# Key and value products in slot 2, the next batch's query product in slot 11, and gate logits from eight columns of the cross products

## What is computed

```python
x = layernorm(x + self_attention(x))      # 16 query heads of 16, one key and value head of 16 for all
qp, kp = proj(x), proj(context)           # proj: two linear maps with biases, one after the other
x = layernorm(x + softmax(qp @ kp.T / 16 + mask) @ context)     # 120 context rows a batch
gate = softmax(x @ Wg.T)                  # 8 experts; the best 2 of each row, scaled to sum 1
x = layernorm(x + sum(gate[e] * (glu(x @ W1[e].T + b1[e]) @ Wo.T + bo) for e in best2))
```

## Time and profile before

| | |
|---|---|
| median of 3 runs | 1420.98 us (1415.15 to 1421.51) |
| the profiled execution | 1420.46 us, span 1418.7 us |
| mean granted TensorE clock | 0.974 |
| first batch's maxima begin | 44.9 us |
| steady steps (7 to 31) | 21.8 us each |
| last exponential of self-attention ends | 786.1 us |
| first expert tile on TensorE | 837.6 us |
| last tile transposed, rows combined | 1242.7 us, 1410.3 us |

### The profile page before, as it was taken

The page is one execution under the profiler, slowest core; times in us unless marked ns, Lnnn a source line. Parts: engine busy times, 40 slices in busy tenths (PEclk is TensorE's granted clock), DMA queues, the critical chain, the costliest instruction groups (busy, mean ns, idle before and its releaser), DMA issues.

```text
span 1418.7 us, 30148 instructions
## 1 busy us (share of the span) xinstructions
PE 1274.8 (90%) x7734; PEld 900.7 (63%) x7735; DVE 1147.8 (81%) x3145; ACT 747.3 (53%) x1740; POOL 642.5 (45%) x978
## 2 busy tenths in 40 slices
PE   6997999999999999999988569999999999968886
PEld 4443555655556555555553357888888888858886
DVE  0565889898888988988986658888888888869998
ACT  1245777777777787777776212233233223314444
POOL 3011354455444554555445323333333333348886
PEclk9998999999999999999999679999999999989999
DMA  7656667667676675775655853433443344379995
GB/s 163 166 111 125 113 151 172 149 163 149 158 157 140 146 163 135 157 138 145 157 129 195 290 215 129 135 130 129 134 135 129 130 134 135 133 271 330 332 335 194
DMA packets 182817, 237.57 MB, mean 167 GB/s; under 512 B 21376, under 2 KB 144256, under 8 KB 176960
## 3 DMA queue, kind: packets, MB, share of 16 engines
q1 hardware_dynamic: 158864, 169.50, 47.3%
q0 software_dynamic: 17488, 55.02, 10.3%
q10 hardware_dynamic: 6368, 11.89, 2.4%
HBM read 138.34 MB, written 98.30 MB: 167 GB/s over the span
## 4 chain that ended last, share of the span: by engine, by line
PE 62%; DVE 17%; issue 9%; DMA 5%; ACT 4%; POOL 1%; SPq 1%; DVEq 0%; ACTq 0%; POOLq 0%
PE psO L623 6%; PE psS L730 5%; PE psHb L1399 5%; PE psHb L1396 5%; PE psHb L1395 4%; PE psHa L1395 4%; PE psHa L1396 4%; PE psHa L1399 4%; PE psB L652 4%; PE psT L740 4%; DVE negmax L1031 3%; DVE x2in L1591 3%; PE psX L1419 2%; DVE gt_lo L1567 2%; PE psA L612 2%
## 5 line engine op out<-in xcount | busy, mean ns | idle before, releaser
L1031 DVE TENSOR_REDUCE negmax<-psS 128x2 f32<-128x512 f32 x512 | 350.7, 688 | 94.6 <-PE psS L730 77.0
L870 ACT ACTIVATE probs<-psT 128x512 f32<-128x512 f32 x512 | 304.0, 599 | 161.0 <-PE psT L740 143.3
L1476 ACT ACTIVATE sig<-hb 128x512 f32<-128x512 f32 x135 | 85.6, 634 | 286.6 <-DVE hb L1549 286.6
L730 PE MATMUL psS<-kstack,qstack 96*128 96x256 bf16 x1024 | 195.2, 273 | 31.3 <-DVE kstack L1129 15.6
L740 PE MATMUL psT<-qstack,kstack 99*128 99x512 bf16 x512 | 194.8, 383 | 4.4 <-ACT probs L870 4.3
L1358 POOL DMA_INDIRECT g_rows<-g,slot x135 | 134.7, 998 | 69.8 <-issue 66.5
L730 PEld LDWEIGHTS psS<-kstack,qstack 96*128 96x128 bf16 x1024 | 93.1, 104 | 90.2 <-DVE negmax L1031 27.4
L482 POOL DMA_INDIRECT lists<-x,slots x128 | 128.6, 1005 | 33.9 <-issue 30.1
L623 PE MATMUL psO<-probs,vaug 128*32 128x512 f32 x1024 | 139.1, 616 | 0.4 <-ACT probs L870 0.4
L1560 DVE SCALAR_TENSOR_TENSOR g<-g,xe,sig 128x512 f32<-128x512 f32 x135 | 101.5, 752 | 26.0 <-DVE g L1556 16.6
L1549 DVE TENSOR_TENSOR hb<-psHb,b 128x512 f32<-128x512 f32 x135 | 93.4, 692 | 33.1 <-issue 28.9
(11 more groups left out here) (207 smaller groups left out, 2956.4 us busy)
## 6 DMA issues: line engine op xcount, KB each, us to landing
rows<-g_rows SPq DMA_DIRECT2D x32, 1024.0 KB, 8.1
qstack<-q_parts SPq DMA_DIRECT2D x192, 128.0 KB
xe<-lists SPq DMA_DIRECT2D x135, 133.0 KB, 2.1
q_parts<-qpart SPq DMA_DIRECT2D x32, 384.0 KB
sums<-x SPq DMA_DIRECT2D x32, 264.0 KB
x2in<-sums SPq DMA_DIRECT2D x32, 264.0 KB, 4.7
xt<-in_x_t SPq DMA_DIRECT2D x32, 256.0 KB
part_raw<-in_f_t SPq DMA_DIRECT2D x32, 256.0 KB, 5.0
```

The costliest lines, as they stand in the source:

```text
L730: last = mm(psS[:, u % 2, hh * S:(hh + 1) * S], qstack[0:KROWS, b1.s4, 2 * hp + hh, c * P:(c + 1) * P], kstack[0:KROWS, b1.s4, :], start=T ...
L870: nc.scalar.activation(probs[:, u % PT, :], psT[:, u % 2, :], ACT.Exp, scale=SELF_SCALE).then_inc(sm["exp_done"], 1)
L1031: v.tensor_reduce(negmax[:, b1.s2, 2 * hp:2 * hp + 2, c], psS[:, u % 2, :].rearrange("p (h k) -> p h k", h=2), AX.X, ALU.max, negate=True) ...
```

## The change

The gate's logits are rstd2 times y2 · wgc, where wgc is wg less its column means, since the norm takes the mean of y2 away and scales it. And y2 is x1 plus the cross-attention's output. So the new kernel never transposes x2. It puts wgc into eight more columns of `keymap`, so that the cross scores' products also give x1 · wgc; it multiplies the context with wgc (two small matmuls on a newly loaded `ctxt`, slot 9) and puts that into eight more columns of `ctxv`; and y2 comes with its eight unscaled logits as columns 256 to 263. Products, copies and norm halves get these slots:

- The pipeline starts one step earlier, and its last step, which only dispatched, is gone: 39 steps, -1 to 37. In step t, q is batch t+1.
- Keys and values of batch t in slot 2, copies in slots 3 and 4, krest in slot 3, third part in slot 7.
- The query of batch t+1 in slot 11, cast and rest in slot 12, the split on POOL behind the rstd of batch t-4 and ahead of mask_b. SP loads xt for t+1 first of all, then stores the query, later loads the stacks.
- The norm to x2 is cut in halves, slots 5 and 6. Gate on VectorE from slot 6 (maxima) and 7 (indices) to 15; exponentials in slots 8 and 9, with rstd2 as scale; counts into psO instead of psB.
- The product with the context uses psA for the first half and psB for the second.
- When draining, the gate runs in slots 1 to 15 and a batch is dispatched and stored at the end of the same step.

The core of the diff; the semaphores' names, the tiles' new sizes (`keymap`, `x1`, `y2`, `ctxv` are eight columns wider, `x2t` and `logits` are gone) and the count per batch of rstd2_ready (4 instead of 3) are left out:

```diff
-        for n in range(B + 7):
+        for n in range(-1, B + 6):
...
+    def count_bank(t):
+
+        return psB if draining(t) else psO[:, 0]
...
-            load_xt(t)
+            load_xt(t.back(-1))
...
+            if active(t):
+                wait(sp, "q1_cast", done(t))
+                wait(sp, "q_split", done(t, 2))
+                sp.dma_start(dram["q"][t.s2].rearrange("t (c p) s -> p t c s", p=P), qpart[:, t.s2]
+                             ).then_inc(sm["q_stored"], 16)
+            if active(t.back(7)) and t.n <= B + 1:
+                store_x2(t.back(7))
...
+                sp.dma_start(ctxt[:, b.s2], io["context_t"][:, b.n * SC:(b.n + 1) * SC].rearrange("(c p) k -> p c k", p=P)
+                             ).then_inc(sm[f"ctxt_loaded{b.s2}"], 16)
...
+            if active(t.back(6)) and draining(t):
+                store_x2(t.back(6))
...
+        def scale_max(b):
+
+            wait(pool, "rstd2_ready", 4 * b.n + 2)
+            pool.tensor_tensor(gneg[:, b.s2], uneg[:, b.s2], rstd2[:, b.s2], ALU.mult).then_inc(sm["rstd2_ready"], 1)
...
+                wait(pool, "gate_exp", done(b6.back(2)))
+                rstd(b6, "var2_ready", mv2, vare2, nmean2, rstd2, shift2, "rstd2_ready", per=4)
+                scale_max(b6)
...
+            late = active(b7) and t.n <= B + 1
+            if late:
                 dispatch(b7, 0)
...
+            if active(q):
+                wait(pool, "q_rest", done(q))
+                wait(pool, "q_stored", done(q.back(2), 16))
+                pool.tensor_tensor(qpart[:, q.s2, 1], qrest[:, q.s2], one_c[:, :].unsqueeze(2).to_broadcast([P, DC, S]),
+                                   ALU.mult).then_inc(sm["q_split"], 1)
+                wait(pool, "q_split", 2 * q.n + 1)
+                pool.tensor_tensor(qpart[:, q.s2, 2], qrest[:, q.s2], qpart[:, q.s2, 1], ALU.subtract
+                                   ).then_inc(sm["q_split"], 1)
...
+            if active(b6) and draining(t):
+                dispatch(b6, 0)
+                dispatch(b6, 1)
...
+            for k in range(DC):
+                mm(psT[:, 0, DC:DC + E], ones[:, :], wg[:, k, :], start=k == 0, stop=k == DC - 1)
...
-        bank_b = {"q_projected": ("q_rest", 0, 1, 1), "x2_transposed": ("x2t_copied", 6, 1, 1),
-                  "gate_scored": ("gate_link", 6, 7, 1), "cprob_transposed": ("cprobt_copied", 5, 1, 1),
-                  "kv_projected": ("k_rest", 0, 1, 1), "counted": ("slot_link", 6, 3, 1)}
+        bank_b = {"kv_projected": ("k_rest", 0, 1, 1), "cprob_transposed": ("cprobt_copied", 5, 1, 1),
+                  "q_projected": ("q_rest", -1, 1, 1), "cross_out": ("y2_ready", 5, 1, 1)}
...
+            if w == 0:
+                wait(pe, "slot_link", 3 * (b.n - 4) + 1)
...
-                if u == 5 and active(b6):
-                    wait(pe, "x2_ready", done(b6))
-                    bank_read(bank_b, t, "x2_transposed")
-                    for c in range(QC):
-                        for k in range(DC):
-                            last = nc.tensor.transpose(psB[:, k * S + c * P:k * S + (c + 1) * P],
-                                                       x2[:, b6.s2, c, k * P:(k + 1) * P], ident[:, :])
-                    last.then_inc(sm["x2_transposed"], 1)
...
-                if u == 7 and active(b6):
-                    wait(pe, "x2t_copied", done(b6))
-                    bank_read(bank_b, t, "gate_scored")
-                    for c in range(QC):
-                        for k in range(DC):
-                            last = mm(psB[:, c * E:(c + 1) * E], x2t[:, b6.s2, k, c * P:(c + 1) * P], wg[:, k, :],
-                                      start=k == 0, stop=k == DC - 1)
-                    last.then_inc(sm["gate_scored"], 1)
...
+                            last = mm(psA[:, c * (SC + E):(c + 1) * (SC + E)], x1t[:, b5.s2, k, c * P:(c + 1) * P],
+                                      keymap[:, k, b5.n, :], start=k == 0, stop=k == DC - 1)
+                    last.then_inc(sm["cross_scored"], 1)
...
+                    if draining(t):
+                        wait(pe, "slot_link", 3 * b6.n + 1)
+                    for c in range(QC):
+                        nc.tensor.transpose(psB[0:SC, c * P:(c + 1) * P], cprob[:, b5.s2, c, :], ident[:, :])
+                    wait(pe, f"ctxt_loaded{b5.s2}", 16 * b5.half + 16)
+                    for k in range(DC):
+                        last = mm(psB[0:SC, S:S + E], ctxt[:, b5.s2, k, :], wgc[:, k, :],
+                                  start=k == 0, stop=k == DC - 1)
+                    last.then_inc(sm["cprob_transposed"], 1)
+                if u == 11 and active(q):
+                    wait(pe, f"xt_loaded{q.s2}", 16 * q.half + 16)
+                    bank_read(bank_b, t, "q_projected")
...
+                    bank_read(bank_b, t, "cross_out")
                     for c in range(QC):
-                        last = mm(psA[:, c * D:(c + 1) * D], cprob_t[:, b5.s2, c * P:(c + 1) * P], ctxv[:, b5.s2, :],
+                        last = mm((psA, psB)[c][:, 0:D + E], cprob_t[:, b5.s2, c * P:(c + 1) * P], ctxv[:, b5.s2, :],
...
-                    bank_read(bank_b, t, "counted")
+                    if draining(t):
+                        bank_read(bank_b, t, "cprob_transposed")
+                    else:
+                        wait(pe, "att_copied", 2 * b3.n + 1)
+                    count = count_bank(t)
...
-                    wait(act, "q_projected", done(t))
-                    wait(act, "q_stored", done(t.back(2), 16))
-                    copy(qpart[:, t.s2, 0].rearrange("p c s -> p (c s)"), psB[:, :]).then_inc(sm["q1_cast"], 1)
-                if u == 4 and active(b6) and not draining(t):
+                    wait(act, "kv_projected", done(t))
+                    wait(act, "pv_done", 4 * (t.n - 3))
+                    wait(act, "scored", UNITS * (t.n - 3))
+                    copy(vaug[:, t.s4, :, 0:DK], psB[:, S:S + QC * DK].rearrange("p (c d) -> p c d", c=QC))
+                    copy(kstack[0:KROWS, t.s4], psB[0:KROWS, 0:S]).then_inc(sm["kv_cast"], 1)
+                if u == 4 and active(t):
+
+                    wait(act, "k_rest", done(t))
+                    copy(kstack[32:64, t.s4], krest[32:64, t.s2])
+                    copy(ksmall[64:80, t.s2], krest[64:80, t.s2]).then_inc(sm["k_mid"], 1)
+                if u in (5, 6) and active(b6) and not draining(t):
                     wait(act, f"x2_stored{b6.s2}", 16 * b6.half)
...
                     wait(act, f"dispatched{b6.s2}", 2 * QC * 16 * b6.half)
-                    norm(x2, rstd2, shift2, y2, b6, "rstd2_ready", "x2_ready")
...
-                    copy(x2t[:, b6.s2].rearrange("p c s -> p (c s)"), psB[:, :]).then_inc(sm["x2t_copied"], 1)
+                    norm(x2, rstd2, shift2, y2, b6, "rstd2_ready", "x2_ready", 4, u - 5)
+                if u in ((6,) if draining(t) else (8, 9)) and active(b6):
+                    wait(act, "gate_max", done(b6))
+                    wait(act, "rstd2_ready", done(b6, 4))
+                    wait(act, "comb_ready", done(b6.back(2)))
+                    for c in range(QC) if draining(t) else (u - 8,):
+                        nc.scalar.activation(gexp[:, b6.s2, c, :], y2[:, b6.s2, c, D:D + E], ACT.Exp,
+                                             scale=rstd2[:, b6.s2, c:c + 1], bias=gneg[:, b6.s2, c:c + 1],
+                                             accum_out=gsum[:, b6.s2, c:c + 1])
+                        last = nc.scalar.activation(gtop[:, b6.s2, c, :], top[:, b6.s2, c, 0:2], ACT.Exp,
+                                                    scale=rstd2[:, b6.s2, c:c + 1], bias=gneg[:, b6.s2, c:c + 1])
...
+                    copy(ctxv[:, b5.s2, D:D + E], psB[0:SC, S:S + E])
                     copy(cprob_t[:, b5.s2], psB[0:SC, 0:S]).then_inc(sm["cprobt_copied"], 1)
...
+                if u == 12 and active(q):
+                    wait(act, "q_projected", done(q))
+                    wait(act, "q_stored", done(q.back(2), 16))
+                    copy(qpart[:, q.s2, 0].rearrange("p c s -> p (c s)"), psB[:, :]).then_inc(sm["q1_cast"], 1)
...
+            v.scalar_tensor_tensor(wgc[:, :, :], psT[:, 0, DC:DC + E].unsqueeze(1).to_broadcast([P, DC, E]), -1.0 / D,
+                                   wg[:, :, :], ALU.mult, ALU.add)
+            for k in range(DC):
+                v.scalar_tensor_tensor(keymap[:, k, :, SC:SC + E],
+                                       psT[:, 0, DC:DC + E].unsqueeze(1).to_broadcast([P, B, E]), -1.0 / D,
+                                       wg[:, k, :].unsqueeze(1).to_broadcast([P, B, E]), ALU.mult, ALU.add)
...
+                    v.tensor_tensor(gneg[:, b6.s2], uneg[:, b6.s2], rstd2[:, b6.s2], ALU.mult
+                                    ).then_inc(sm["rstd2_ready"], 1)
...
+            if at(6, 1):
+                for c in range(QC):
+                    last = v.max(top[:, b.s2, c, :], y2[:, b.s2, c, D:D + E])
```

(46 more changed lines are left out.)

360 lines of the change are left out of this document (144 added, 216 removed).

## The result

| | before | changed |
|---|---|---|
| median | 1417.52 us (10 runs, 1409.81 to 1421.96) | 1427.31 us (10 runs, 1422.19 to 1435.02) |
| ratio to before | | 1.0071, 95% interval 1.0047 to 1.0095 |
| profiled execution, span | 1420.46, 1418.7 | 1435.02, 1433.1 |
| step 6 begins (the 1st is numbered 1) | 158.8 | 151.0 |
| steps 6 to 31, 26 of them | 571.0 | 591.0 |

The profiled execution is the longest of its ten. By step 6 the changed kernel is 7.8 us ahead, prologue included, where 9.8 were forecast. The steady steps lost 20 us, where 13.5 were to be gained, and the drain lost 2.7.

What follows compares the result with a forecast made beforehand. No engine was taken as full; how slots chain sets the step. Terms +4.4 - 14.2 - 13.5 - 2 - 2 = -27.3 us, from 1420.98 to 1394 us, range 1368 to 1412, chance 0.42.

Steps and rivals of the forecast that it cites:

- Prologue, +4.4: Before the first step: query product ahead of the fold 2.9 us, `ones` product 0.5, VectorE instructions 0.95; sum +4.4 us.
- Filling steps, -14.2: Steps 1 to 5: stalls and low clock go, -14.2 us, or half if ScalarE's exponentials are the next wait.
- Steady steps, -0.5 each: Steps 6 to 32: 0.2 us less to cprob_t's copy, 0.3 less in VectorE's part; -13.5 us, between 0 and -40.
- rival D: Steady steps, slots 3 and 4: casts and krest wait for each other, cprob_t over 0.5 us later; 1436 us, chance 0.07.
- named as late next: Slots 0 to 2: first normalization's chain, from moments in slot 13, sets the x1 transpose; no shrinking taken there.
- Rival C: Steady steps gain zero: ScalarE in slots 3 to 9 delays cprob_t and the query product; 1408 to 1415 us, chance 0.28.
- POOL against VectorE, 0: Moved split: mpart gains 0.47 us, gexp scalings lose 0 to 0.6 each; set at 0, at worst 0.7 a step.
- Draining, -2 and -2: Steps 33 and 34 lose 1 us each; steps 35 to 37 save 2 us, since DMA is nearly full.
- A step of 21.3 us: Steady steps: the length named as a sign that the forecast is right, against 21.8 us before.

Runs made afterwards that it cites:

- the run with the later dispatches: Changed kernel with GpSimd's four dispatches of a draining step moved behind the next step's power for rstd; 1423.52 us, ratio 1.0043.
- the second profile of before: The kernel before, unchanged, profiled a second time; span 1418.1 us.
- the balanced kernel: Changed kernel with gate exponentials in slot 11, key casts in 8, third key part in 9, draining dispatches behind the next step's power; 1391.93 us, ratio 0.983.
- the exchange alone: Kernel before with only the products exchanged (keys and values in slot 2, next batch's query in slot 11), old gate kept; 1490.17 us, ratio 1.0508.
- the gate alone: Changed kernel with the products put back (query in slot 2, keys and values in slot 11), new gate kept; 1424.86 us, ratio 1.0057.
- the run with mrows first: Changed kernel with ScalarE's copy of mrows in slot 6 instead of 7, ahead of the x2 norm's second half; 1423.28 us, ratio 1.0057.
- the later split: The balanced kernel with GpSimd's split of the query product behind mask_b instead of ahead of it; 1389.33 us, ratio 0.9827.

## Why the prediction was wrong, point by point

- **Prologue, +4.4: nothing to show for it.** The first part is there: the fold's product with itself (`wc`) begins at 27.73 us with the change (in the run with the later dispatches) and at 23.92 in the second profile of before, 3.8 us later. But it takes 1.99 us instead of 3.64, and the first context map 3.46 instead of 5.16, in a stretch at a clock of 1.00 where it was 0.83 (24 to 34 us). The term was priced at one clock, and the query product in it at 1.73 us where it takes 3.75 here; the sum depends on which stretch runs at 1.2 GHz, and profiles of the same prologue differ by 5 us.
- **Filling steps, -14.2: 9.7 between the two own profiles, 14.6 between the second profile of before and that with the later dispatches.** Steps 3 to 5 came as forecast (3.3 + 4.2 + 2.6 against 3.8 + 4.0 + 2.1 us). Steps 1 and 2 were to gain 4.1 us; the one lost 1.0, the other gained 0.8: in place of the waits for kstack and xt TensorE kept 1.06 us at the end of each, for negmax, which stands behind the copy of keybias, and got new ones for the context groups (1.27 and 0.58 us, for DMAs). The next wait took over here, as the bound had it, though for these two steps alone, and it was not ScalarE's exponentials.
- **Steady steps, -0.5 each: +0.62, the step that failed.** The forecast cut a step at the third exponential and at the end of the copy of cprob_t, and both parts failed.
  - *The first part, 9.57 us before, was to be 9.4 and is 9.90.* ScalarE's work in it was forecast as 9.4 and is 9.38. What failed is to take the length of a full in-order queue to be its work: the queue itself waits 0.45 us for krest, and this wait stood in rival D and not in the sum. What stands in the queue on the way comes late too: mrows (0.82 us of waiting for TensorE), the exponential of slot 5 (0.47), cprob_t (0.27). None of these waits has a row in the prediction but the last, though the copy of mrows in slot 7 stands behind all that was put into slots 3 to 6. That this queue sets the part is shown: with the casts and gate exponentials elsewhere it takes 8.75 us.
  - *The other part, 12.25 us before, was to lose 0.3 and grew by 0.3.* It did so by the same amount in the balanced kernel, so moving work out of ScalarE's first slots doesn't touch it. 0.33 us of it stand ahead of the third exponential: TensorE waits 0.38 us for the x1 norm, which was named as late next. In the steady steps that wait is in every kernel with the exchanged products (0.3 to 0.4 us a step), and the kernels without the exchange show it once in all. In the table, slots 11 to 13 grow from 2.79 to 3.20 us in the changed kernel and with the exchange alone, and not with the gate alone. So it comes with the query product in slot 11. (From slot 14 to the next step's slot 0 the changed kernel gains 0.36 us, where the third key part is gone.) A likely reason is that VectorE does qrest (0.69 us and a wait of 0.25) ahead of the moments of y1, where krest (0.42) stood; no run moved it.
- **What the low clock costs** wasn't in the sum. Before, none of the 26 steps had a clock under 1.00 (one in the second profile). With the change six had 0.93 in its own profile and were 1.1 to 1.8 us longer, three in the run with the later dispatches, none in the run with mrows first. That is 4 to 7 us.
- **Rival D was the right one,** with 0.07. Its threshold was a step of 22.3 us and its place ScalarE's slots 3 to 9. With the measured 22.44 its own sum gives 1421 + 27 x 0.62 - 9.8 - 2 = 1426, against 1427.31. Its condition, casts and krest waiting for each other, is the row of 0.45 us, and the copy of cprob_t ends 0.67 us later in the step than before, where it had said over 0.5. Part of the match in us is luck: its -9.8 and -2 for fill and drain were -7.8 and +2.7 in the profiles, and the profiled execution lies 7.7 us over the median that the sum is held against. It also left out the other part's +0.3 us. Rival C was the same queue with a smaller price. What stood against both was 0.2 us, 9.4 of 9.6, which was too little ground for a chance of 0.42 against 0.35.
- **POOL against VectorE, 0.** mpart fell from 0.66 to 0.18 us and the scalings rose from 0.22 to 0.39 each, and these two were indeed near each other, 0.48 against 0.33. The rule of the Trainium skill (SBUF — State Buffer, "Who interferes with whom") held for the instructions: the scaling that began during the first split, or with it, ended within 0.03 us of the split's end (0.56 us, and 1.08 with the later split), and the one begun 0.15 us ahead of it took its 0.22 us. The forecast's 0.7 us a step for it is in no run: the loss falls in slot 15, and there it is covered.
- **Draining, -2 and -2: +2.7 between the own profiles** (111.9 us from step 32 to the first expert product, 114.6 with the change), and some 5 us over all profiles (108.0 to 111.9 without it, 113.2 to 115.9 with it). The mistake was on POOL's queue. The dispatches of batch t-6 were seen to move to the end of their own step, but not that the power of the next step stands behind the last of them: 3.5 to 4.3 us of VectorE's chain in each of four steps. The other bound, DMA, fits: of the 8 us that the later dispatches took out of the chain, some 2 to 3 counted, at a DMA share of 0.90. That it was DMA which kept the rest back was not tested.
- **A step of 21.3 us exists:** it is the balanced kernel's, 21.29. That it equals the forecast's is luck: the forecast had 9.4 and 11.9 us for the two parts, and it is 8.75 and 12.54. The idea of the change holds; two casts, a third part and two pairs of exponentials stood in the wrong slots.
